# Storing three by three maxima instead of row maxima of five, and pooling every class of planes from them

## The chip, the cores and the metric

The kernel runs on one core of a Trainium2 chip. The metric is the device time of one execution in microseconds (us); runs are compared by their medians. The engines are named as in the profile: PE (matrix), DVE (vector), ACT (scalar), POOL (the fourth compute engine, which also issues the indirect DMAs) and SP (which issues the other DMAs).

## The reference

The input x has 16 images of 512 channels of 64 by 64 pixels, in float32. Layer 0 normalises x in groups of 16 channels, computes at each pixel the correlation with its 25 neighbours, divides these by their norm, and sends 512 + 25 channels through a one by one convolution with ReLU; its result is added to x and gives y. Layer 1 normalises y in groups and scores each of the 8192 planes (image and channel); the score picks two neighbouring pool sizes, and the result is their weighted sum. Cut to what matters here:

```
KERNELS = (1, 3, 5, 7, 9, 11, 13)
s = relu(score(b, c));  q_s = clip(floor(s), 0, 5);  q_b = q_s + 1
pools = [maxpool_same(y, k) for k in KERNELS]
y = y + (s - q_s) * pools[q_b] + (q_b - s) * pools[q_s] + groupnorm(y)
```

(The pools are taken of the normalised y, which is y scaled and shifted per plane with a positive factor, so the kernel takes them of y.)

## The kernel before

The second stage groups the planes by class q_s (0 to 5) into 67 tiles of 128 planes, one plane in a partition, and 5 empty tiles fill up to 72. The first stage makes y, and prepares for the second.

**First stage.** A loop over 16 images, each with 8 chunks of 8 rows (512 pixels for each of the 4 channel tiles of 128). Images 0, 14 and 15 are written out; the 13 between them are one turn of a DVE loop each, and PE's loop has a turn for seven. PE does for each chunk, in this order: `picks` (L1241), the products `gram` 0 and 1 of the next chunk (L1196), `tail` of the chunk before (L1274), `norm` (L1263), `gram` 2 and 3, one part of the convolution (L1219 to L1221), `turn_blocks` (L1254), and the other three parts. `gram` t waits until the mask of t - 2 is done, since two PSUM banks alternate: so `gram` 2 of a chunk waits for the first mask of that chunk.

DVE does for each chunk, in this order: `x_stats` (four BATCH_NORM_STATS2, L739; in all chunks but chunk 5), masks 0 and 1 (L789), `descriptor` (L831, L835, which wait for ACT's square root L617, which waits for `norm`), mask 2, the four `y_stats` (L801) with mask 3 between them, in chunk 0 `keep_stats`, in chunk 3 a second `x_stats`, then `wide_rows` for the chunk before, and in chunk 4 `group_spreads` and `group_values`, of which PE's `group_spread` (L1286) waits for L762. The y statistics wait for POOL's `residual` (L448), whose third and fourth part come after POOL's `halves`, which waits for `descriptor`. After `residual`, POOL does the subtraction L439 for the fourth channel tile of the chunk three ahead; those of the first three tiles come in the next chunk, as soon as ACT has made their inputs (L580, L582). In chunk 5 all four come behind `residual`.

`wide_rows` (L803) takes the maximum of five neighbours in a row, clamped at the ends, in six maxima over the 4 channel tiles at once (L810, L812, L817, L820, L822, L825). It puts pair maxima into `pairs_m`, whose space is shared with ACT's `relu`, and the result into the one buffer `wide`, which SP stores to `wide_planes` (L377, 1 MB). `s_middle` is raised after the third, `s_wide` after the last. The third waits for the store of the chunk before.

**Second stage.** For tile t, POOL gathers 128 planes of y (L507) and their records (L504) into one of four `bufs`, and the row maxima into one of two `source` buffers (L523), two tiles ahead; tiles of class 0 and 1 pool from y itself, and their `source` gather has out-of-range indices in all partitions but one, which fetch nothing. DVE's `pools` (all at L1039) makes the smaller pool in `small` and the larger in `big`, two buffers of each. ACT puts the scaled plane into the 8 PSUM banks (L665), PE adds diag times `small` (L1390; not in class 0) and diag times `big` (L1392) bank by bank, ACT copies the banks out (L679), and POOL scatters the result to `out` (L530). ACT takes tile t + 1 in only when all banks of tile t are out.

In class 0 `pools` takes seven maxima of half a plane and makes `big` (3 by 3). In class 1 two whole-plane maxima follow. In class 2 it makes five by five from the row maxima in four half-plane maxima, and then two whole-plane maxima for seven by seven. In classes 3 to 5 it widens the row maxima (three to six maxima), takes column maxima in `window`, and grows that by one. Outer rows and columns of `hbuf`, `small` and `source` are padded with the lowest float.

## Time and profile before

| | |
|---|---|
| median of 3 runs | 4183.77 us (4174.26 to 4189.22) |
| profiled execution: its time, its span | 4180.08 us, 4177.9 us |
| PE busy | 3474.2 us, 83% of the span |
| DVE busy | 3378.0 us, 81% |
| ACT, POOL busy | 1981.8 us, 2087.4 us |
| mean granted clock of PE | 0.919 of full |
| DMA moved | 782.10 MB, mean 187 GB/s |

The span runs from the first to the last instruction. The first stage ends at about 2550 us, the sorting of the planes at 2608 us, and the first maximum of the second stage starts at 2618.01 us. Busy times are shares of the whole span and mix the two stages; which engine is waited for has to be read in each stage by itself.

### The profile page before, as it was taken

The page shows a single profiled execution, that of the slowest core. Times are in us where ns is not written, and L with a number is a line of the kernel's source. Part 1 is how long each engine was busy: PE and PEld are TensorE (multiplying, and loading weights), DVE is VectorE, ACT ScalarE, POOL GpSimd, SP SyncE. Part 2 cuts the span into 40 slices and gives each one's busy share as a digit, 9 for nine tenths or more (in the row PEclk, how much of TensorE's full clock was granted, in tenths as well). Part 3 has the DMA queues.
Part 4 walks back from the last instruction along what each step waited for, and adds up shares of the span by engine and source line. Part 5 has one row for each costly group of instructions (what it writes and reads, how often), then busy time and mean ns, then how long its engine had stood idle before and what let it go on. Part 6 is the DMA issues. An engine that isn't in the chain of part 4 may idle for free. (4 is left out here: it accounts for less than half of the span.)

```text
span 4177.9 us, 72982 instructions
## 1 busy us (share of the span) xinstructions
PE 3474.2 (83%) x22600; PEld 1981.8 (47%) x22601; DVE 3378.0 (81%) x3619; ACT 1981.8 (47%) x3227; POOL 2087.4 (50%) x1576
## 2 busy tenths in 40 slices
PE   4999999999999999999999996567678666666554
PEld 3666666666665666666666664223233222222221
DVE  5777777777777777777777766899989999999995
ACT  3545445445445545545445440664556544444342
POOL 3555555556555555555555541554444444454343
PEclk9999999999999999999999996878889888877777
DMA  5445445445454454455455233664478666565552
GB/s 195 154 156 185 164 157 187 158 164 181 161 175 168 165 176 166 162 177 178 147 177 187 98 128 74 258 244 186 184 293 339 269 254 244 232 247 197 222 199 81
DMA packets 252355, 782.10 MB, mean 187 GB/s; under 512 B 98150, under 2 KB 98150, under 8 KB 229990
## 3 DMA queue, kind: packets, MB, share of 16 engines
q1 hardware_dynamic: 219600, 417.85, 29.0%
q0 software_dynamic: 32288, 358.95, 21.9%
q8 instruction: 181, 2.97, 0.3%
q14 instruction: 286, 2.34, 0.2%
HBM read 428.22 MB, written 409.08 MB: 200 GB/s over the span
## 5 line engine op out<-in xcount | busy, mean ns | idle before, releaser
L1039 DVE TENSOR_TENSOR arena<-arena 128x2048 f32<-128x2048 f32 (+9 forms) x635 | 1454.8, 2319 | 66.4 <-issue 23.1
L439 POOL TENSOR_TENSOR arena<-arena 128x512 f16<-128x512 f32 x512 | 651.2, 1277 | 861.5 <-ACT arena L582 860.3
L1390 PE MATMUL psum<-arena 128*128 128x512 f32 x896 | 534.9, 682 | 461.5 <-issue 336.6
L448 POOL TENSOR_TENSOR arena<-arena 128x512 f32 (+1 forms) x512 | 639.7, 1271 | 293.6 <-ACT arena L594 288.2
L1219 PE MATMUL psum<-arena 128*128 128x512 f16 x2048 | 776.3, 379 | 1.0 <-ACT arena L594 1.0
L1221 PE MATMUL psum<-arena 128*128 128x512 f16 x2048 | 776.2, 379 | 0.0
L1220 PE MATMUL psum<-arena 128*128 128x512 f16 x2048 | 776.2, 379 | 0.0
L1196 PE MATMUL psum<-arena 128*128 128x256 f16 (+1 forms) x6344 | 712.7, 270 | 34.5 <-DVE arena L789 21.2
L580 ACT ACTIVATE arena<-arena,gbias,grstd 128x512 f32 (+1 forms) x512 | 413.7, 808 | 632.0 <-PE psum L1221 515.6
L1392 PE MATMUL psum<-arena 128*128 128x512 f32 x1072 | 604.5, 661 | 71.1 <-ACT psum L665 54.4
L679 ACT ACTIVATE arena<-psum 128x512 f32<-128x512 f32 x536 | 315.9, 598 | 716.4 <-PE psum L1392 704.4
L1196 PEld LDWEIGHTS psum<-arena 128*128 128x128 f16 x6344 | 589.2, 99 | 118.9 <-DVE arena L789 29.4
L801 DVE BATCH_NORM_STATS2 bny<-arena 128x6 f32 (+1 forms) x512 | 354.3, 693 | 286.8 <-POOL arena L448 282.0
L530 POOL DMA_INDIRECT out<-arena x67 | 179.1, 2674 | 763.3 <-issue 763.3
L1390 PEld LDWEIGHTS psum<-arena 128*128 128x128 f32 x896 | 188.5, 218 | 724.3 <-issue 574.5
L594 ACT ACTIVATE arena<-psum,bias_sb 128x512 f32<-128x512 f32 x512 | 338.0, 686 | 217.7 <-POOL arena L448 205.8
L1392 PEld LDWEIGHTS psum<-arena 128*128 128x128 f32 x1072 | 230.3, 216 | 387.3 <-issue 320.9
L582 ACT ACTIVATE arena<-arena,gbias,grstd 128x512 f16 (+1 forms) x512 | 409.4, 800 | 0.0
L665 ACT ACTIVATE psum<-arena 128x512 f32<-128x512 f32 x536 | 383.3, 767 | 47.8 <-ACT arena L679 47.6
L739 DVE BATCH_NORM_STATS2 bnx<-arena 128x6 f32 (+1 forms) x512 | 314.8, 679 | 36.2 <-issue 25.2
L789 DVE TENSOR_TENSOR arena<-psum,cst 128x256 f32<-128x256 f32 x496 | 276.5, 587 | 79.3 <-PE psum L1196 78.9
L1221 PEld LDWEIGHTS psum<-arena 128*128 128x128 f16 x2048 | 200.4, 98 | 241.7 <-issue 0.2
(150 smaller groups left out, 3246.6 us busy)
## 6 DMA issues: line engine op xcount, KB each, us to landing
arena<-in_x SPq DMA_DIRECT2D x64, 2048.0 KB, 13.0
wide_planes<-arena SPq DMA_DIRECT2D x128, 1024.0 KB, 8.9
y_planes<-arena SPq DMA_DIRECT2D x64, 2048.0 KB, 7.7
arena<-arena SPq DMA_DIRECT2D x1536, 8.0 KB, 1.8
arena<-wide_planes,arena POOLq DMA_INDIRECT x72, 11.7
arena<-plane_records,arena POOLq DMA_INDIRECT x67, 7.8
arena<-y_planes,arena POOLq DMA_INDIRECT x67, 9.7
out<-arena POOLq DMA_INDIRECT x67, 9.2
```

The source lines that it names most:

```text
L439: pool.tensor_tensor(gl[:, ct, slot], g32[:, ct % 2, :], gh[:, ct, slot], ALU.subtract).then_inc(s_gl, 1)
L448: pool.tensor_tensor(y, y, relu[:, o % 2, :], ALU.add).then_inc(s_added, 1)
L580: act.activation(g32[:, ct % 2, :], piece, ACT.Identity, bias=gbias[:, ct:ct + 1], scale=grstd[:, ct:ct + 1])
L582: act.activation(gh[:, ct, (c % RING) * CW:(c % RING + 1) * CW], piece, ACT.Identity, bias=gbias[:, ct:ct + 1], scale=grstd[:, ct:ct + 1]) ...
L665: act.activation(psum[:, b, :], bufs[:, u, b * CW:(b + 1) * CW], ACT.Identity, bias=recs_in[:, u, 3:4], scale=recs_in[:, u, 0:1]).then_inc ...
L1039: ins = dve.tensor_tensor(dst, a, b, ALU.max)
L1196: return pe.matmul(dst, w, m, start=(k == 0), stop=(k == nk - 1))
L1219: pe.matmul(dst, h, gh[:, ct, slot], start=(ct == 0), stop=False)
L1220: pe.matmul(dst, h, gl[:, ct, slot], start=False, stop=False)
L1221: last = pe.matmul(dst, l, gh[:, ct, slot], start=False, stop=(ct == CT - 1))
L1390: pe.matmul(dst, diag[:, s, 0, :], small[:, s, b * ROWS:(b + 1) * ROWS, 1:W + 1], start=False, stop=False, skip_group_check=True)
L1392: pe.matmul(dst, diag[:, s, 1, :], big[:, s, b * CW:(b + 1) * CW], start=False, stop=True, skip_group_check=True).then_inc(s_mix, 1)
```

## The change

The first stage no longer stores row maxima of five, but three by three maxima, with the even columns of a row first and then the odd ones. Since the last row of a chunk needs the first of the next, chunk 0 stores 7 rows, chunk 7 stores 9, and the others 8 that start one row higher (`wide_span`). The work goes over two channel tiles at a time, and in chunk 7 over one, with seven maxima for each turn (eight in chunks 0 and 7): 14 maxima in chunks 1 to 6, 16 in chunk 0 and 32 in chunk 7. `column` takes the place of `pairs_m` in the space of `relu`. Every maximum of `wide_rows` now comes behind the wait for the store, and ACT waits for `s_wide` where it waited for `s_middle`.

In the second stage all classes gather these maxima, into three `source` buffers. Class 0 gives them to PE as they are, so that `pools` has nothing to do. Class 1 gives them to PE as the smaller pool and makes five by five with `grown` (one pixel wider on each side). Class 2 grows twice; classes 3 to 5 make seven, nine and eleven directly and grow that. PE reads planes in the split column order and writes each column to its place in PSUM, with a step of two elements. The diff, cut to its core:

```diff
-source = v(2 * (H + 2 * PADY) * W).rearrange("p (s h w) -> p s h w", s=2, w=W)
-hbuf_f = v((H + 2 * PADR) * W)
-hbuf = hbuf_f.rearrange("p (h w) -> p h w", w=W)
-small_f = v(2 * H * (W + 2))
-small = small_f.rearrange("p (s h w) -> p s h w", s=2, h=H)
-big = v(2 * PIX).rearrange("p (s n) -> p s n", s=2)
-half_m = v(36 * W)
+source = v(SRC * PIX).rearrange("p (s h w) -> p s h w", s=SRC, w=W)
+hbuf = v((H + 2) * W).rearrange("p (h w) -> p h w", w=W)
+small = v(2 * PIX).rearrange("p (s h w) -> p s h w", s=2, w=W)
+big = v(2 * PIX).rearrange("p (s h w) -> p s h w", s=2, w=W)
...
+def wide_span(c):
+    return max(c * ROWS - 1, 0), H if c == CH - 1 else (c + 1) * ROWS - 1
...
-        sp.dma_start(wide_v[bass.ds(i, 1), :, :, c * CW:(c + 1) * CW].rearrange("b p t n -> p (b t) n"),
-                     wide_f.rearrange("p (t n) -> p t n", t=CT)).then_inc(wide_stored, 16)
+        first, top = wide_span(c)
+        sp.dma_start(wide_v[bass.ds(i, 1), :, :, first * W:top * W].rearrange("b p t n -> p (b t) n"),
+                     wide_f.rearrange("p (t n) -> p t n", t=CT)[:, :, 0:(top - first) * W])\
+          .then_inc(wide_stored, 16)
...
-        sp.wait_ge(s_wide, i * CH + 2 * q + 2)
+        sp.wait_ge(s_wide, i * CH + min(2 * q + 3, CH))
...
-        if t >= 2:
-            pool.wait_ge(s_rows, t - 1)
-            pool.wait_ge(sourced[b % 2], t // 2 * 16)
-        pool.indirect_dma_start(out=source_flat(b % 2), out_offset=None, in_=wide_dram[:, :],
+    def gather_source(t):
+        if t >= SRC:
+            pool.wait_ge(sourced[t % SRC], t // SRC * 16)
...
-            act.wait_ge(s_middle, chunk)
+            act.wait_ge(s_wide, chunk)
...
+        def op(dst, a, b, wait=True, signal=s_pairs):
+            if wait and used[0]:
+                dve.wait_ge(s_pairs, n * PAIR_OPS + used[0])
+            dve.tensor_tensor(dst, a, b, ALU.max).then_inc(signal, 1)
+            if signal is s_pairs:
+                used[0] += 1
+        first, top = wide_span(c)
+        total = top - first
+        r = max(first, 1)
+        np_ = (min(top, H - 1) - r) // 2
         dve.wait_ge(s_added, (n + 1) * CT)
-        dve.tensor_tensor(pairs_m[:, :, :, 1:half], y[:, :, :, 1:W - 2:2], y[:, :, :, 2:W - 1:2], ALU.max)\
-            .then_inc(s_pairs, 1)
-        dve.tensor_tensor(pairs_m[:, :, :, 0:half + 1:half], y[:, :, :, 0:W:W - 1], y[:, :, :, 0:W:W - 1],
-                          ALU.max).then_inc(s_pairs, 1)
-        dve.wait_ge(s_pairs, n * 4 + 2)
         if not (isinstance(n, int) and n == 0):
             dve.wait_ge(wide_stored, n * 16)
-        dve.tensor_tensor(wide[:, :, :, 0:W:2], pairs_m[:, :, :, 0:half], pairs_m[:, :, :, 1:half + 1],
-                          ALU.max).then_inc(s_middle, 1)
-        dve.wait_ge(s_middle, n + 1)
-        dve.tensor_tensor(wide[:, :, :, 1:W - 2:2], wide[:, :, :, 0:W - 3:2], y[:, :, :, 3:W:2], ALU.max)\
-            .then_inc(s_pairs, 1)
-        dve.tensor_tensor(wide[:, :, :, W - 1:W], wide[:, :, :, W - 2:W - 1], wide[:, :, :, W - 2:W - 1],
-                          ALU.max).then_inc(s_pairs, 1)
-        dve.wait_ge(s_pairs, n * 4 + 4)
-        dve.tensor_tensor(wide[:, :, :, 2:W:2], wide[:, :, :, 2:W:2], y[:, :, :, 0:W - 3:2], ALU.max)\
-            .then_inc(s_wide, 1)
+        step = 1 if total > ROWS else 2
+        for t in range(0, CT, step):
+            ts = slice(t, t + step)
+            pairs = wide[:, ts, 0:np_, :]
+            column = relu_f[:, 0:step * total * W].rearrange("p (t h w) -> p t h w", t=step, w=W)
+            inner = column[:, :, r - first:r - first + 2 * np_, :]
+            op(pairs, y[:, ts, r:r + 2 * np_:2, :], y[:, ts, r + 1:r + 1 + 2 * np_:2, :])
+            op(inner[:, :, 0::2, :], pairs, y[:, ts, r - 1:r - 1 + 2 * np_:2, :])
+            op(inner[:, :, 1::2, :], pairs, y[:, ts, r + 2:r + 1 + 2 * np_:2, :], wait=False)
+            if c == 0:
+                op(column[:, :, 0:1, :], y[:, ts, 0:1, :], y[:, ts, 1:2, :], wait=False)
+            if c == CH - 1:
+                op(column[:, :, total - 1:total, :], y[:, ts, H - 2:H - 1, :], y[:, ts, H - 1:H, :], wait=False)
+            even, odd = wide[:, ts, 0:total, 0:W // 2], wide[:, ts, 0:total, W // 2:W]
+            op(odd, column[:, :, :, 0::2], column[:, :, :, 1::2])
+            op(even[:, :, :, 0:1], odd[:, :, :, 0:1], odd[:, :, :, 0:1])
+            op(even[:, :, :, 1:], odd[:, :, :, 1:], column[:, :, :, 1:W - 2:2], wait=False)
+            done = t + step == CT
+            op(odd[:, :, :, 0:W // 2 - 1], odd[:, :, :, 0:W // 2 - 1], column[:, :, :, 2::2],
+               signal=s_wide if done else s_pairs)
+        assert used[0] <= PAIR_OPS
+        dve.sem_inc(s_pairs, PAIR_OPS - used[0])
...
-        link(dve.tensor_scalar(sel, tcls, 2.0, None, ALU.is_ge))
-        link(dve.scalar_tensor_tensor(sel, tcls, float(NCLS), sel, ALU.is_lt, ALU.mult))
+        link(dve.tensor_scalar(sel, tcls, float(NCLS), None, ALU.is_lt))
...
+        def split(a):
+            return a.rearrange("p h (e j) -> p h e j", e=2)
+        def grown(src, dst, signal=s_own):
+            even, odd = split(src)[:, :, 0, :], split(src)[:, :, 1, :]
+            h_even, h_odd = split(inner)[:, :, 0, :], split(inner)[:, :, 1, :]
+            op(h_even[:, :, 1:], odd[:, :, 0:31], odd[:, :, 1:])
+            op(h_odd[:, :, 0:31], even[:, :, 0:31], even[:, :, 1:], wait=False)
+            op(h_even[:, :, 0:1], odd[:, :, 0:1], odd[:, :, 0:1], wait=False)
+            op(h_odd[:, :, 31:], even[:, :, 31:], even[:, :, 31:], wait=False)
+            op(dst, hbuf[:, 0:H, :], hbuf[:, 2:H + 2, :], signal=signal)
+        threes = source[:, u % SRC, :, :]
+        sm_, bg = small[:, s, :, :], big[:, s, :, :]
+        inner = hbuf[:, 1:H + 1, :]
+        even, odd = split(threes)[:, :, 0, :], split(threes)[:, :, 1, :]
+        h_even, h_odd = split(inner)[:, :, 0, :], split(inner)[:, :, 1, :]
+        def edge(a, n):
+            return a.to_broadcast([P, H, n])
+        def edge_row(r, n):
+            return inner[:, r:r + 1, :].to_broadcast([P, n, W])
+        if k == 2:
+            grown(threes, sm_)
+        elif k == 3:
+            m = split(bg)[:, :, 0, :]
+            tw = lambda a: a.rearrange("p h (e j) -> p (h e) j", e=2)
+            op(m[:, :, 1:31], odd[:, :, 0:30], even[:, :, 2:])
+            op(tw(inner)[:, :, 0:32:31], tw(threes)[:, :, 0:31:30], tw(threes)[:, :, 1:32:30], wait=False)
+            op(h_even[:, :, 1:31], m[:, :, 1:31], even[:, :, 0:30])
+            op(h_odd[:, :, 1:31], m[:, :, 1:31], odd[:, :, 2:], wait=False)
+            m = bg[:, 1:31, :]
+            two = lambda a: a.rearrange("p (a b) w -> p a b w", b=2)
+            op(m, inner[:, 1:60:2, :], inner[:, 4:63:2, :])
+            op(two(sm_)[:, 0:32:31, :, :], two(inner)[:, 0:32:31, :, :], two(inner)[:, 1:31:29, :, :], wait=False)
+            op(sm_[:, 2:61:2, :], m, inner[:, 0:59:2, :])
+            op(sm_[:, 3:62:2, :], m, inner[:, 5:64:2, :], wait=False)
+        elif k == 4:
+            m = split(bg)[:, :, 0, :]
+            op(m[:, :, 0:31], even[:, :, 0:31], odd[:, :, 1:])
+            op(h_odd[:, :, 0:1], odd[:, :, 0:1], even[:, :, 2:3], wait=False)
+            op(h_even[:, :, 31:], even[:, :, 31:], odd[:, :, 29:30], wait=False)
+            op(h_even[:, :, 2:31], m[:, :, 2:31], odd[:, :, 0:29])
+            op(h_odd[:, :, 1:30], m[:, :, 0:29], even[:, :, 3:], wait=False)
+            op(h_even[:, :, 0:2], m[:, :, 0:2], edge(odd[:, :, 0:1], 2), wait=False)
+            op(h_odd[:, :, 30:], m[:, :, 29:31], edge(odd[:, :, 31:], 2), wait=False)
+            m = bg[:, 0:31, :]
+            op(m, inner[:, 0:61:2, :], inner[:, 3:64:2, :])
+            op(sm_[:, 1:2, :], inner[:, 1:2, :], inner[:, 4:5, :], wait=False)
+            op(sm_[:, 62:63, :], inner[:, 62:63, :], inner[:, 59:60, :], wait=False)
+            op(sm_[:, 4:61:2, :], m[:, 2:31, :], inner[:, 1:58:2, :])
+            op(sm_[:, 3:60:2, :], m[:, 0:29, :], inner[:, 6:63:2, :], wait=False)
+            op(sm_[:, 0:3:2, :], m[:, 0:2, :], edge_row(1, 2), wait=False)
+            op(sm_[:, 61:64:2, :], m[:, 29:31, :], edge_row(63, 2), wait=False)
+        elif k == 5:
+            q_even, q_odd = split(bg)[:, :, 0, :], split(bg)[:, :, 1, :]
+            op(q_even[:, :, 0:31], even[:, :, 0:31], odd[:, :, 1:])
+            op(q_odd[:, :, 0:30], odd[:, :, 0:30], even[:, :, 2:], wait=False)
+            op(h_even[:, :, 2:30], q_even[:, :, 0:28], q_odd[:, :, 2:30])
+            op(h_odd[:, :, 2:30], q_odd[:, :, 0:28], q_even[:, :, 3:31], wait=False)
+            op(h_even[:, :, 0:2], q_odd[:, :, 0:2], edge(odd[:, :, 0:1], 2), wait=False)
+            op(h_odd[:, :, 0:2], q_even[:, :, 1:3], edge(odd[:, :, 0:1], 2), wait=False)
+            op(h_even[:, :, 30:], q_even[:, :, 28:30], edge(even[:, :, 31:], 2), wait=False)
+            op(h_odd[:, :, 30:], q_odd[:, :, 28:30], edge(even[:, :, 31:], 2), wait=False)
+            q = bg[:, 0:61, :]
+            op(q, inner[:, 0:61, :], inner[:, 3:64, :])
+            op(sm_[:, 4:60, :], q[:, 0:56, :], q[:, 5:61, :])
+            op(sm_[:, 0:4, :], q[:, 1:5, :], edge_row(1, 4), wait=False)
+            op(sm_[:, 60:64, :], q[:, 56:60, :], edge_row(62, 4), wait=False)
+        grown(threes if k == 1 else sm_, bg, signal=s_pool)
...
+                    if not (isinstance(t, int) and t < 2):
+                        dve.wait_ge(s_mix, (t - 1) * 8)
+                    dve.wait_ge(sourced[u % SRC], wide_loaded)
...
+                pe.wait_ge(sourced[u % SRC], wide_loaded)
+                mix_banks(t, s, [(1, threes)])
             with pe.Else():
-                mix_banks(t, u, s, True)
+                with pe.If(cls_t < 2):
+                    mix_banks(t, s, [(0, threes), (1, big[:, s, :, :])])
+                with pe.Else():
+                    mix_banks(t, s, [(0, small[:, s, :, :]), (1, big[:, s, :, :])])
...
-    def mix_banks(t, u, s, with_small):
+    def mix_banks(t, s, terms):
         for b in range(8):
             pe.wait_ge(s_first, t * 8 + b + 1)
-            dst = psum[:, b, :]
-            if with_small:
-                pe.matmul(dst, diag[:, s, 0, :], small[:, s, b * ROWS:(b + 1) * ROWS, 1:W + 1],
-                          start=False, stop=False, skip_group_check=True)
-            pe.matmul(dst, diag[:, s, 1, :], big[:, s, b * CW:(b + 1) * CW], start=False, stop=True,
-                      skip_group_check=True).then_inc(s_mix, 1)
+            dst = psum[:, b, :].rearrange("p (h j e) -> p h e j", h=ROWS, e=2)
+            for k, plane in terms:
+                rows = plane[:, b * ROWS:(b + 1) * ROWS, :].rearrange("p h (e j) -> p h e j", e=2)
+                last = pe.matmul(dst, diag[:, s, k, :], rows, start=False, stop=k == 1, skip_group_check=True)
+            last.then_inc(s_mix, 1)
```

## Rows read from the trace of the kernel before

**Rows 1.** Windows of the four stretches (columns as in the first row), core 0.
```profile
core 0: us, PE busy (x) PEld busy (x) DVE busy (x) ACT busy (x) POOL busy (x), PEclk, DMA share, GB/s
95.00:2540.00 2445.00, 2389.98 (x20125) 1498.31 (x20123) 1826.14 (x2772) 1184.62 (x1884) 1342.26 (x1256) 1.00 0.47 163
2618.00:2775.00 157.00, 89.73 (x160) 36.61 (x160) 150.16 (x77) 112.42 (x193) 82.31 (x39) 0.80 0.68 265
3278.00:4120.00 842.00, 517.70 (x1024) 217.93 (x1024) 811.97 (x379) 363.61 (x608) 387.31 (x128) 0.80 0.57 223
```

**Rows 2.** Timeline of DVE, a plain chunk: start, us, engine line, [idle before <-releaser].
```profile
1490.83 2.07 DVE L810 TENSOR_TENSOR arena<-arena 128x992 f32 x1
...
1493.23 1.23 DVE L817 TENSOR_TENSOR arena<-arena 128x1024 f32<-128x1024 f32 x1
1494.68 1.20 DVE L820 TENSOR_TENSOR arena<-arena 128x992 f32<-128x992 f32 x1 [0.22 <-DVE arena L817]
1495.79 0.22 DVE L822 TENSOR_TENSOR arena<-arena 128x32 f32<-128x32 f32 x1
1496.22 1.19 DVE L825 TENSOR_TENSOR arena<-arena 128x992 f32<-128x992 f32 x1 [0.20 <-DVE arena L822]
1497.33 2.46 DVE L739 BATCH_NORM_STATS2 bnx<-arena 128x6 f32 x4
1499.71 1.02 DVE L789 TENSOR_TENSOR arena<-psum,cst 128x256 f32<-128x256 f32 x2
```

**Rows 3.** Timeline of ACT: the square roots that follow norm, in four chunks.
```profile
1461.94 0.37 ACT L617 ACTIVATE arena<-psum,epsd 128x128 f32<-128x128 f32 x1 [0.30 <-PE psum L1263]
...
1482.98 0.37 ACT L617 ACTIVATE arena<-psum,epsd 128x128 f32<-128x128 f32 x1 [0.64 <-PE psum L1263]
...
1539.71 0.37 ACT L617 ACTIVATE arena<-psum,epsd 128x128 f32<-128x128 f32 x1 [0.17 <-PE psum L1263]
...
1560.86 0.37 ACT L617 ACTIVATE arena<-psum,epsd 128x128 f32<-128x128 f32 x1 [4.37 <-PE psum L1263]
```

**Rows 4.** Timelines of DVE and PE behind a turn of DVE's loop.
```profile
1457.66 1.19 DVE L825 TENSOR_TENSOR arena<-arena 128x992 f32<-128x992 f32 x1 [0.22 <-DVE arena L822]
1460.85 2.47 DVE L739 BATCH_NORM_STATS2 bnx<-arena 128x6 f32 x4 [2.00 <-issue]
1463.24 1.02 DVE L789 TENSOR_TENSOR arena<-psum,cst 128x256 f32<-128x256 f32 x2
...
1463.87 2.79 PE L1196 MATMUL psum<-arena 128*128 128x256 f16 x24 [1.97 <-DVE arena L789]
```

**Rows 5.** Timeline of DVE in chunk 4: the last row maximum and what PE waits for.
```profile
1553.04 1.19 DVE L825 TENSOR_TENSOR arena<-arena 128x992 f32<-128x992 f32 x1 [0.22 <-DVE arena L822]
...
1554.73 0.16 DVE L762 TENSOR_TENSOR gd<-gd,aggx 128x4 f32<-128x4 f32 x1
```

**Rows 6.** Timeline of POOL in the plain chunk of rows 2.
```profile
1490.70 1.16 POOL L439 TENSOR_TENSOR arena<-arena 128x512 f16<-128x512 f32 x1 [0.68 <-ACT arena L582]
1498.32 1.16 POOL L439 TENSOR_TENSOR arena<-arena 128x512 f16<-128x512 f32 x1 [6.46 <-ACT arena L582]
```

**Rows 7.** Timeline of DVE in the second stage: a tile of class 1, of class 2 in two parts.
```profile
2799.14 22.89 DVE L1039 TENSOR_TENSOR arena<-arena 128x2048 f32<-128x2048 f32 x9 [0.16 <-DVE arena L1039]
...
3149.24 9.21 DVE L1039 TENSOR_TENSOR arena<-arena 128x2112 f32<-128x2112 f32 x4
3158.60 8.88 DVE L1039 TENSOR_TENSOR arena<-arena 128x4096 f32<-128x4096 f32 x2 [0.15 <-DVE arena L1039]
```

**Rows 8.** Timeline of PE, two tiles of class 2.
```profile
3151.17 1.63 PE L1390 MATMUL psum<-arena 128*128 128x512 f32 x2 [2.21 <-ACT psum L665]
...
3165.84 1.02 PE L1392 MATMUL psum<-arena 128*128 128x512 f32 x2
3169.08 1.13 PE L1390 MATMUL psum<-arena 128*128 128x512 f32 x2 [2.22 <-ACT psum L665]
```

**Rows 9.** Windows: five microseconds in which DMA is full, columns as in rows 1.
```profile
3155.00:3160.00 5.00, 5.00 (x13) 2.25 (x12) 4.85 (x3) 3.52 (x8) 4.27 (x3) 0.99 1.02 387
```

**Rows 10.** Timeline of PE: products that write PSUM with a step.
```profile
1291.22 0.60 PE L1254 MATMUL psum<-cst,arena 128*128 128x128 f32 x4
...
1459.79 1.89 PE L1274 MATMUL psum<-arena 96*128 96x256 f16 x8
```

**Rows 11.** Store of the row maxima: all 128 of them, time from issue to landing.
```profile
DMA to landing us min/median/max: 4.2/8.9/16.2
```

136 lines of the change are left out of this document (28 added, 108 removed).

## The prediction

> **What bounds the kernel now.** I read the windows first, since the shares of the whole span mix two stages. In the first stage PE is busy 2390 of 2445 us at the full clock, DVE 1826 [rows 1]: PE is the bound, and the 619 us in which DVE idles look like room. In the second stage DVE is busy 812 of 842 us in classes 3 to 5 [rows 1], and its timeline has 0.15 us between tiles in classes 1 and 2 [rows 7]: there DVE is the bound. In class 2 PE follows closely, at one tile in 17.9 us (3151.17 to 3169.08) [rows 8] against DVE's 9.21 + 8.88 us and gaps, 18.4 [rows 7]. In class 0 DVE has 150 of 157 us and DMA a share of 0.68 [rows 1].
>
> Idle time is not room if it stands between two waits, so I read the timeline of one chunk for what comes after what. I name R the end of the square root L617. Five intervals carry the first stage:
> - R to the first row maximum: 7.5 us (1483.35 to 1490.83) [rows 2, 3]. It is a chain over ACT, POOL and DVE (ReLU, residual, halves, residual, statistics), which a faster or slower `wide_rows` doesn't touch. In chunk 0 `keep_stats` makes it 9.6, in chunk 3 the second `x_stats` 9.9.
> - `wide_rows` itself, W: 1490.83 to 1497.41, 6.6 us [rows 2].
> - its end to the end of mask 0: `x_stats` and one mask of 0.59, 1497.41 to 1500.3, 2.9 us [rows 2]; 5.0 behind the turn of DVE's loop (1458.85 to 1463.83) [rows 4].
> - mask 0 late: `gram` 2 starts as soon as it is done (1463.87, after 1.97 us idle), and the next R comes at 1483.35, 19.5 us behind the mask [rows 3, 4]. R itself is not late, since `norm` stands ahead of `gram` 2.
> - chunk 4: 7.0 us from the end of `wide_rows` (1554.23) to the next R (1561.23), since `group_spread` waits for L762, four small instructions behind it [rows 3, 5].
>
> When nothing is late, R comes every 18.9 us. So for two plain chunks in a row: 2 x 18.9 = 37.8 is the least, and 7.5 + W + 2.9 + 19.5 = 29.9 + W is what DVE allows. W may be 7.9 at most; now it is 6.6. That is all the room that the 619 us hold in a plain chunk. In chunk 4 there is none now.
>
> **First part: `wide_rows` is longer.** Before, 4096 elements in a partition in 6 maxima. After, chunks 1 to 6: per turn 512 x 4 + 16 + 496 x 2 = 3056, times 2 = 6112, in 14. One element takes 1/0.96 ns: 992 take 1.11 us when the next maximum doesn't wait (0.08 on top) and 1024 take 1.45 when it waits and forms an address in the loop (0.38 on top); a small one takes 0.43 [rows 2]. A wait without an address costs 0.19 on top, by the whole-plane maxima of the second stage (8.88 for two) [rows 7]. So 6.37 + 3 x 0.38 + 6 x 0.2 + 4 x 0.1 + 0.3 = 9.4 us without interference, where the old ones make 5.7. Chunk 0: 5212 elements, 8.7. Chunk 7 in four turns: 6748 elements and 32 maxima, 13.8.
>
> Interference is on top. L810 took 2.07 us here against 1.19 for L825 of as many elements, while L439 of POOL, begun at 1490.70, ran until 1491.86 [rows 2, 6]: 0.9 us. The next L439 begins at 1498.32, 0.9 us after the old `wide_rows` has ended, and well inside the new one. I take one further collision of 0.9 in each chunk that has subtractions there; the bounds are none and three. The Trainium skill (SBUF — State Buffer, Who interferes with whom) states that a DVE instruction with two SBUF inputs and a POOL instruction that reads SBUF exclude each other for a whole instruction. The 0.9 us agree. By that rule each of the three L439 (the third is due some 19 us after R) that meets the chain would cost a whole one, which is the upper bound here.
>
> In a plain chunk W is then 9.4 + 0.9 + 0.9 = 11.2, and 29.9 + 11.2 = 41.1 for two chunks instead of 37.8. With a late mask the 7.5 us are no longer exact: the chain through `descriptor` and `halves` gives 5.8 us from mask 0 to the first maximum, if that is later. Followed through one image (W; late mask after R; period): chunk 0: 14.7; 4.4; 23.9. Chunk 1: 9.6; 5.9; 25.4. Chunk 2: 11.2; none; 18.9. Chunk 3: 10.3; 2.7; 22.2. Chunk 4: 10.3; 1.8; 7.6 + 10.3 + 7.0 = 24.9. Chunk 5 (no `x_stats`, four subtractions): 12.8; none; 18.9. Chunk 6: 9.8; 4.3; 23.0. Chunk 7: 10.8; none; 19.1. Sum 176.3. The same rules give 153.6 for the old lengths. So +22.7 us for an image in the loop, +19.0 without a further collision (172.6), +30.8 with all three (184.4). For 13 images 295. In the three written out no addresses are formed (9.4 becomes about 8.8) and no loop turns: I estimate 14 each, 42, with the end, where the last `wide_rows` also waits for a store first. First stage: +337, bounds +280 and +450.
>
> The store moves in front of all maxima. It lands 4.2 to 16.2 us after issue, 8.9 in the median [rows 11]; with W at 11 it has 12 us or so until the next begins. The slow ones queue behind a load and a store issued earlier, so their landing stays where it is in time, and I cost it at nothing beside a late start; if they took their 15 us from the later issue, some 9 us an image, 120 in all. ACT's wait for `s_wide` costs nothing where mask 0 is late anyhow, since both wait for the same end. SP's loads wait for a chunk that the store issued before them has already waited for. Behind SP's wait for the store stand the regroup DMAs, which wait for `halves` some 3.5 us after R; even in chunk 1 the maxima end before that (26.9 - 23.9 = 3.0). The bytes stored stay the same.
>
> **Second part: `pools`.** `grown` is 2 x 1984, 2 x 64 and 4096 elements: 2.14 x 2 + 0.5 + 4.44 = 9.2 us [rows 2, 7].
> - Class 0: DVE does nothing. But a tile now moves three times 2.10 MB, 6.29 MB, where it moved two. DMA gives 387 GB/s when full [rows 9]: 16.3 us a tile; PE and ACT need about 10 (half of 15.7, and 2.2) [rows 8]. Before 14.4 (2618.0 to 2776.1, the latter from the first row of rows 7 less two tiles of class 1, for 11 tiles). The loss of 1.9 x 11 = 21 is given back by the start, where 14 us of maxima no longer stand before PE's first product, and by 8 products at the end: together -2. The Trainium skill (SBUF — State Buffer, A bandwidth-pool intuition that's wrong) gives 358 GB/s for HBM to a core; that would be 17.6 us a tile and 14 us more in all. The 387 of the trace stands against it.
> - Class 1: DVE 9.4, DMA 16.3, PE and ACT 17.6 (17.9, and half a microsecond less in a tile that starts at the full clock, as 1.13 stands to 1.63 in rows 8). Against 22.89 + 0.16 [rows 7]: 11 x 5.5 = -61.
> - Class 2: 18.5 against 18.4: +1.
> - Classes 3, 4, 5: with elements/0.96 and 0.15 for each maximum, 20224, 20352 and 24192 elements in 13, 19 and 17 maxima make 23.0, 24.15 and 27.9 us. The old sizes by the same rule make 24.6, 25.65 and 28.4, which gives 837 of the 842 us window [rows 1]. So 11 x -1.6, 11 x -1.5, 10 x -0.5: -39.
> PE's longer way through the branches and the fewer paddings are under 2 us and cancel. Second stage: -2 - 61 + 1 - 39 = -101, bounds -80 and -130 (class 1 at the 16.3 of DMA).
>
> **PE writes PSUM with a step of two.** L1274, in f16, writes with a step: 8 products of 256 columns take 1.89 us, where 24 of L1196 without one take 2.79 [rows 4, 10], so 0.22 against 0.11 each. L1254, in f32, has a step of 16 and takes 0.11 us for 128 columns (0.60 for 4, the last 0.27 long) [rows 10], 0.85 ns a column, as the f32 records of the mix do (15.7 us for 32 of 512 columns, 0.43 at the full clock) [rows 8]. The mix is f32, nearest to L1254: no cost. The other bound is a rival.
>
> **The sum.** 4180.1 + 337 - 101 = 4416. The profiled execution is 3.7 us (0.1%) below the median of the runs shown, so I keep 4415, +5.5%. 0.3% is about what a measurement of this kernel tells from no change.
>
> **The rivals.**
> - Faster: the longer `wide_rows` fits into DVE's 619 us, and PE keeps 18.9. For it: 128 x 3.7 = 474 us is less than 619. Against it: the place of the idle time, and `gram` 2 that already waited 1.97 us for a mask [rows 4]. It decides where W is under 7.9 in a plain chunk, and 6112 elements take 6.4 us without any overhead. Then 4183.8 - 101 = 4083. Chance 0.10.
> - Half the loss: part of the 7.5 us chain or of `x_stats` gives way. +15 an image and 25, 220 in all less 101: 4300. Chance 0.10.
> - All subtractions collide, or the stores land 15 us behind their later issue, or PE's longer idle time lowers its clock (it was 1.00 in the first stage and 0.80 in class 0, where PE idles 40% [rows 1]): 4183.8 + 450 - 101 = 4530. Chance 0.16.
> - The step costs PE double: 27.4 + 2.2 = 29.6 us for each tile of classes 1 to 5, so 12, 11, 6.6, 5.5 and 1.7 us more on 11, 13, 11, 11 and 10 tiles, 426 in all: 4840. Chance 0.10.
> - My forecast, 4415, by itself 4350 to 4480: 0.54.
>
> The range 4250 to 4540 leaves out the first and the fourth. Faster by over 0.3% 0.10, within 0.3% 0.02, slower 0.88.
>
> **What the changed profile would show.** The first stage is right if L739 starts directly behind the last maximum, PE idles ahead of `gram` 2 in chunks 0, 1, 3 and 6, L617 comes every 22 us in the mean, and PE waits 5 us or more for L762; wrong if PE is busy 98% there. W is right at 9.4 to 11.2. The second stage is right if the DMA share is near 1 in class 0, tiles of class 1 take 17.6 us with DVE half idle, and a pair of products stays at 1.02. What would make it wrong most easily is W, since each microsecond of it is worth half a microsecond in a plain chunk and a whole one in chunk 4.

## Result and the profile after

The changed kernel takes 4628.84 us (median of 4 runs, 4624.27 to 4631.09) against 4185.63 (median of 4, 4174.26 to 4189.22): a ratio of 1.106 (95% interval 1.104 to 1.109). The forecast was 4415, in a range of 4250 to 4540. The direction was right, the size was not. The profiled execution took 4631.09 us, with a span of 4629.3; before, 4180.08 and 4177.9.

Windows of the changed kernel: the first stage, class 0, classes 3 to 5, and below them a wait of PE, the four microseconds behind it, and five later ones of the same chunk. Columns as in [rows 1].

```profile
core 0: us, PE busy (x) PEld busy (x) DVE busy (x) ACT busy (x) POOL busy (x), PEclk, DMA share, GB/s
95.00:3060.00 2965.00, 2520.06 (x19833) 1565.18 (x19832) 2385.01 (x4028) 1180.49 (x1867) 1344.44 (x1237) 0.91 0.37 133
3196.00:3342.00 146.00, 92.69 (x155) 37.88 (x156) 0.00 (x0) 101.42 (x182) 37.30 (x37) 0.75 1.00 420
3760.00:4585.00 825.00, 536.21 (x1061) 226.44 (x1062) 797.88 (x533) 380.78 (x638) 348.21 (x136) 0.81 0.60 239
1818.00:1826.00 8.00, 0.00 (x0) 0.00 (x0) 6.93 (x16) 2.00 (x4) 2.47 (x3) 0.69 0.43 168
1826.00:1830.00 4.00, 3.62 (x18) 2.56 (x19) 2.66 (x6) 0.88 (x2) 2.41 (x4) 0.50 0.33 122
1838.00:1843.00 5.00, 5.00 (x68) 2.48 (x66) 4.30 (x10) 0.32 (x1) 0.15 (x1) 1.00 0.99 364
```

From the first R to the last, the first stage takes 3018.0 us instead of 2451.7, 566 more. (The windows can't be subtracted for this: this one ends 26 us before the last R, that of [rows 1] 20 us behind it.) In the windows PE is no longer busy 98% of the time but 85%. DVE is busy 2385 us and still idles 580: neither engine is full in the mean, as before. The waits say who stops whom. Waits of PE, 200 to 3000 us: line waited for, total, times, longest.

```profile
PE psum L1203 <- DVE arena L786: 397.5, 72, 8.6
PE psum L1293 <- DVE gd L759: 31.9, 14, 3.0
```

L1203 is `gram` (L1196 before), L786 the mask (L789), L1293 `group_spread`. In 72 chunks PE stands before `gram` 2 for the first mask, 5.5 us in the mean.

One plain chunk, timelines of DVE, POOL, PE and ACT. The maxima of `wide_rows` are now L812, the subtraction L440, the square root L614, `x_stats` L736.

```profile
1660.53 0.69 DVE L798 BATCH_NORM_STATS2 bny<-arena 128x6 f32 x1 [0.54 <-POOL arena L449]
1661.14 1.59 DVE L812 TENSOR_TENSOR arena<-arena 128x512 f32 x1
1662.94 3.54 DVE L812 TENSOR_TENSOR arena<-arena 128x512 f32<-128x512 f32 x6 [0.21 <-DVE arena L812]
1667.21 0.69 DVE L812 TENSOR_TENSOR arena<-arena 128x512 f32 x1 [0.73 <-DVE arena L812]
1668.11 6.17 DVE L812 TENSOR_TENSOR arena<-arena 128x512 f32<-128x512 f32 x6 [0.21 <-DVE arena L812]
1674.20 2.47 DVE L736 BATCH_NORM_STATS2 bnx<-arena 128x6 f32 x4
1676.58 1.02 DVE L786 TENSOR_TENSOR arena<-psum,cst 128x256 f32<-128x256 f32 x2
```
```profile
1661.02 1.16 POOL L440 TENSOR_TENSOR arena<-arena 128x512 f16<-128x512 f32 x1 [0.70 <-ACT arena L579]
1668.64 1.19 POOL L440 TENSOR_TENSOR arena<-arena 128x512 f16<-128x512 f32 x1 [6.46 <-ACT arena L579]
1670.05 1.34 POOL L440 TENSOR_TENSOR arena<-arena 128x512 f16<-128x512 f32 x1 [0.23 <-ACT arena L579]
1671.66 1.28 POOL L440 TENSOR_TENSOR arena<-arena 128x512 f16<-128x512 f32 x1 [0.28 <-ACT arena L579]
```
```profile
1677.21 3.17 PE L1203 MATMUL psum<-arena 128*128 128x256 f16 x14 [5.05 <-DVE arena L786]
```
```profile
1653.27 0.37 ACT L614 ACTIVATE arena<-psum,epsd 128x128 f32<-128x128 f32 x1 [0.63 <-PE psum L1270]
1672.20 0.37 ACT L614 ACTIVATE arena<-psum,epsd 128x128 f32<-128x128 f32 x1 [0.61 <-PE psum L1270]
1698.17 0.37 ACT L614 ACTIVATE arena<-psum,epsd 128x128 f32<-128x128 f32 x1 [0.54 <-PE psum L1270]
```

The five intervals of the prediction can be read off. R is 1653.64 (1653.27 + 0.37), the first maximum comes 7.5 us later, `wide_rows` lasts to 1674.28, so W = 13.1, the mask is done at 1677.2, 2.9 behind it and 4.6 behind the next R (1672.57); `gram` 2 waited 5.05 us. All four subtractions lie inside `wide_rows`. The R after that comes at 1698.54, 26.0 us after its predecessor, while the pair started with one of 18.9. The mean of the 13 images in the loop, from the first R of one to the first R of the next, is 194.3 us (before: 155.3; the prediction's rules gave 176.3 and 153.6).

The second stage, from the last R to the end of the span, takes 1542.9 us instead of 1657.8: 115 us less. Tiles of class 1, timeline of DVE (L1055 is every maximum of `pools`) and PE (L1402, both products):

```profile
3368.57 9.25 DVE L1055 TENSOR_TENSOR arena<-arena 128x1984 f32<-128x1984 f32 x5 [6.25 <-DMA arena<-wide_planes,arena]
3384.04 9.24 DVE L1055 TENSOR_TENSOR arena<-arena 128x1984 f32<-128x1984 f32 x5 [6.22 <-DMA arena<-wide_planes,arena]
```
```profile
3381.80 14.00 PE L1402 MATMUL psum<-arena 128*128 128x512 f32 x32 [2.22 <-ACT psum L662]
```

DVE is busy 9.25 us in a tile where it was 22.89 [rows 7]. PE's 32 products take 14.0 us with the step of two, at a granted clock of 1.00; in the kernel before the 32 of the tile of class 2 that starts at 3169.08 take 14.0 us without the step, at 1.00 as well.

### The profile page after: what moved, and what is told of

Read it like the earlier page. It is cut to its first block and busy times, and to the rows that moved or that the text cites. A ratio compares the mean times of both kernels' runs of the same rounds, so it can differ in the third digit from the quotient of the medians.

```text
span 4629.3 us, 75558 instructions
## 1 busy us (share of the span) xinstructions
PE 3626.9 (78%) x22600; PEld 2064.7 (45%) x22601; DVE 3642.6 (79%) x5029; ACT 1976.8 (43%) x3227; POOL 2003.2 (43%) x1576
## 5 line engine op out<-in xcount | busy, mean ns | idle before, releaser
L812 DVE TENSOR_TENSOR arena<-arena 128x512 f32<-128x512 f32 (+11 forms) x2112 | 1392.8, 686 | 150.8 <-DVE arena L812 102.7
L1055 DVE TENSOR_TENSOR arena<-arena 128x64 f32<-128x64 f32 (+8 forms) x707 | 1119.5, 1636 | 275.5 <-DMA arena<-wide_planes,arena 210.8
L1402 PE MATMUL psum<-arena 128*128 128x512 f32 x1968 | 983.5, 663 | 421.8 <-ACT psum L662 266.8
L1203 PE MATMUL psum<-arena 128*128 128x256 f16 (+1 forms) x6344 | 855.6, 302 | 421.8 <-DVE arena L786 409.0
L440 POOL TENSOR_TENSOR arena<-arena 128x512 f16<-128x512 f32 x512 | 666.1, 1304 | 1095.7 <-ACT arena L579 1093.9
L1203 PEld LDWEIGHTS psum<-arena 128*128 128x128 f16 x6344 | 660.7, 110 | 579.3 <-DVE arena L786 423.7
L1402 PEld LDWEIGHTS psum<-arena 128*128 128x128 f32 x1968 | 414.5, 214 | 990.7 <-issue 706.4
L676 ACT ACTIVATE arena<-psum 128x512 f32<-128x512 f32 x536 | 305.0, 603 | 547.9 <-PE psum L1402 535.3
L591 ACT ACTIVATE arena<-psum,bias_sb 128x512 f32<-128x512 f32 x512 | 337.9, 686 | 379.0 <-POOL arena L449 205.6
L527 POOL DMA_INDIRECT out<-arena x67 | 167.2, 2495 | 749.2 <-issue 749.2
L798 DVE BATCH_NORM_STATS2 bny<-arena 128x6 f32 (+1 forms) x512 | 338.6, 682 | 134.5 <-POOL arena L449 131.5
L786 DVE TENSOR_TENSOR arena<-psum,cst 128x256 f32<-128x256 f32 x496 | 276.4, 587 | 196.6 <-PE psum L1203 196.5
L736 DVE BATCH_NORM_STATS2 bnx<-arena 128x6 f32 (+1 forms) x512 | 314.9, 678 | 38.2 <-issue 27.2
L1228 PEld LDWEIGHTS psum<-arena 128*128 128x128 f16 x2048 | 201.3, 98 | 244.7 <-issue 5.4
L1226 PEld LDWEIGHTS psum<-arena 128*128 128x128 f16 x2048 | 203.5, 99 | 215.3 <-issue 4.7
```

Of the source, the lines that this page charges most:

```text
L440: pool.tensor_tensor(gl[:, ct, slot], g32[:, ct % 2, :], gh[:, ct, slot], ALU.subtract).then_inc(s_gl, 1)
L812: dve.tensor_tensor(dst, a, b, ALU.max).then_inc(signal, 1)
L1055: ins = dve.tensor_tensor(dst, a, b, ALU.max)
L1203: return pe.matmul(dst, w, m, start=(k == 0), stop=(k == nk - 1))
L1226: pe.matmul(dst, h, gh[:, ct, slot], start=(ct == 0), stop=False)
L1228: last = pe.matmul(dst, l, gh[:, ct, slot], start=False, stop=(ct == CT - 1))
```

## The experiments

In the table "pace" is the mean time of an image over the 13 in the loop, read from the square roots of each trace, and "W, sum" the lengths of the eight `wide_rows` of an image added up, in the same 13 (in e6 those of its halves). e1, e2 and e4 are one execution each; repeated runs of one kernel here stay within 0.5% of each other.

| run | us | pace | W, sum | from last R to the end |
|---|---|---|---|---|
| before | 4181 to 4186 | 155.3 | 53.7 | 1657.8 |
| changed | 4628.8 | 194.3 | 97.9 | 1542.9 |
| e1, before, one maximum twice | 4259.6 | 161.9 | 65.8 | 1646.4 |
| e2, before, one maximum four times | 4648.3 | 187.0 | 93.5 | 1662.3 |
| e3, changed, half the maxima | 4069.6 | 155.4 | 42.5 | 1539.6 |
| e4, changed, no subtraction | 4345.3 | 175.1 | 77.8 | 1546.5 |
| e5, changed, later `x_stats` | 4525.6 | 187.2 | 98.1 | 1546.7 |
| e6, e5 and half of `wide_rows` later | 4522.9 | 185.3 | 91.1 | 1545.2 |
| e7, e5 without subtraction | 4279.6 | 170.8 | 77.8 | 1544.6 |
| e8, changed, filler on PE | 4603.6 | 192.4 | 99.3 | 1542.5 |
| e9, changed, long filler | 4614.0 | 191.4 | 99.3 | 1544.1 |
| e10, before, no subtraction | 4169.8 | 154.7 | 48.2 | 1658.1 |

**Is it the length of `wide_rows`?** Two doses on the kernel before. One of its maxima is repeated, with the same operands and result:

```diff
+for j in range(1):          # e2: 3
+    dve.wait_ge(s_pairs, n * 5 + 4 + j)
+    dve.tensor_tensor(wide[:, :, :, 1:W - 2:2], wide[:, :, :, 0:W - 3:2], y[:, :, :, 3:W:2], ALU.max)\
+        .then_inc(s_pairs, 1)
```

> The kernel before, with one of the six maxima of wide_rows (L820, 992 elements in a partition) made a second time with the same values, so W grows by about 1.5 us, to 8.1. The store, its wait and ACT's wait for s_middle stay as they are. Theory (DVE works in order, so a longer wide_rows makes mask 0 late once W is over 7.9 in a plain chunk, and at once in chunk 4): 5 to 9 us more for an image, 4260 to 4340 in all, and PE waiting for masks by several times the 1.97 us of a chunk that it waited before. Rival (DVE has 619 us of room in the first stage): 4184. Rival (what cost time in the changed kernel is the wait for the store or ACT's wait for s_wide, not the length): 4184.

> The kernel before, with the maximum L820 made four times in place of once, W about 11.1 us, as long as in the changed kernel. Theory: about 19 us more for an image without collisions with POOL and 30 with them, so 4490 to 4700, and in a plain chunk with a late mask the square root comes 19.5 us or more behind mask 0. If the drop of PE's granted clock belongs to the idle time, it shows here too (below 0.95 in the first stage). Rivals as in the run with one repetition: 4184 both.

Measured: 4259.6 and 4648.3 us, one execution each, beside 4181.8 for the kernel before (median of 7). What PE waits for, from 200 to 2400 us, first with one repetition, then with three:

```profile
PE psum L1200 <- DVE arena L789: 82.3, 39, 2.3
PE psum L1290 <- DVE gd L762: 10.0, 6, 1.7
```
```profile
PE psum L1200 <- DVE arena L789: 247.1, 62, 6.4
PE psum L1290 <- DVE gd L762: 43.1, 11, 4.5
```

Unchanged, the kernel before has 21.2 us of the first wait in the same window, 24 times. With nothing but a longer `wide_rows` it loses 78 and 466 us, the first 0.4 us below the range expected, the second inside it. Both rivals gave 4184 and fall. With three repetitions the granted clock of PE is 0.93 in the first stage, below 0.95 as expected. The slope is instructive. The first repetition makes `wide_rows` 12.0 us longer in an image and costs 6.7; the next two make it 27.8 us longer (two maxima in each of eight chunks are some 24, the rest is waits and subtractions that now lie beside it) and cost 25.0. Below the room of 7.9 us a part is free; over it a microsecond of W costs 0.9, not the half that the prediction put on a plain chunk. At 93.5 us of W this kernel has a pace of 187.0, and the changed one with 97.9 has 194.3: length explains most of the loss.

**Do the waits cost, or the maxima?** The changed kernel with the maxima of channel tiles 2 and 3 alone, all waits and stores kept:

```diff
-for t in range(0, CT, step):
+for t in range(CT // 2, CT, step):
```

> The changed kernel, with the maxima of the first stage made for channel tiles 2 and 3 alone (in chunk 7 the same), so that W is about 5 us; the other half of wide_planes holds zeros, and the output is not the reference's. Every wait and every store stays. Theory (the loss is the length of wide_rows): the first stage takes as long as before, and the second keeps its gain of about 125 us: 4040 to 4080. Rival (the wait for the store in front of all maxima, or ACT's wait for s_wide, cost time by themselves): over 4150. The second stage by itself: 120 to 130 us less than before.

Measured: 4069.6 us, ratio 0.974 (0.972 to 0.975), within what was expected. The pace is that of before. So the wait for the store in front of all maxima, the loads that wait longer, and ACT's wait for `s_wide` cost nothing where W is short (42.5 us an image). The run doesn't show what they cost at the full W, since a short W also gives the store more time to land and ends ACT's wait early. The second stage, from the last R, is 118 us shorter by itself; 120 to 130 were expected.

**The subtractions.** The changed kernel with L440 made for 8 of 512 columns:

```diff
-pool.tensor_tensor(gl[:, ct, slot], g32[:, ct % 2, :], gh[:, ct, slot], ALU.subtract).then_inc(s_gl, 1)
+few = slice((c % RING) * CW, (c % RING) * CW + 8)
+pool.tensor_tensor(gl[:, ct, few], g32[:, ct % 2, 0:8], gh[:, ct, few], ALU.subtract).then_inc(s_gl, 1)
```

> The changed kernel, with the subtraction of POOL (L440) made for 8 of 512 columns; the rest of the low parts is zero, so the convolution is less precise and the output is not the reference's. It takes away the work of POOL that runs beside the maxima of DVE and nothing else. Theory (each of the subtractions that meets wide_rows costs DVE 0.9 us, three or more in a plain chunk): W falls from about 11.2 to 9.4 us, an image gets 12 us shorter or more, 4380 to 4450 in all. Rival (waits and addresses make W long, POOL does not matter): W stays over 10.5 and the time over 4580.

Measured: 4345.3 us (one execution), 283 less than the changed kernel and below the range expected. The same chunk of the same image as above, timeline of DVE (L817 are the maxima, L741 `x_stats`):

```profile
1510.93 0.68 DVE L817 TENSOR_TENSOR arena<-arena 128x512 f32 x1
1511.82 3.55 DVE L817 TENSOR_TENSOR arena<-arena 128x512 f32<-128x512 f32 x6 [0.21 <-DVE arena L817]
1516.09 0.69 DVE L817 TENSOR_TENSOR arena<-arena 128x512 f32 x1 [0.73 <-DVE arena L817]
1517.00 3.57 DVE L817 TENSOR_TENSOR arena<-arena 128x512 f32<-128x512 f32 x6 [0.21 <-DVE arena L817]
1520.49 2.46 DVE L741 BATCH_NORM_STATS2 bnx<-arena 128x6 f32 x4
```

W is 9.6 instead of 13.1. The lines that differ are those over which a subtraction lay: 0.68 against 1.59, one subtraction; 3.57 against 6.17, three. Each adds 0.87 to 0.91 us. Over all 2112 maxima, first the changed kernel, then this one:

```profile
L812 DVE TENSOR_TENSOR arena<-arena 128x512 f32<-128x512 f32 (+11 forms) x2112 | 1392.8, 686 | 150.8 <-DVE arena L812 102.7 <-DMA wide_planes<-arena 9.5 <-issue 6.0
```
```profile
L817 DVE TENSOR_TENSOR arena<-arena 128x512 f32<-128x512 f32 (+11 forms) x2112 | 1089.3, 542 | 177.7 <-DVE arena L817 102.6 <-DMA wide_planes<-arena 36.6 <-issue 5.8
```

303.5 us less, 19.0 for each of the 16 images (W in the loop falls by 20.0), and the pace falls by 19.2. The two lines also show DVE's wait for the store: 9.5 us in all in the changed kernel, and 36.6 in this one, where DVE is ready for it earlier. So the collisions hid a part of that wait, and it is small in both.

**The control on the kernel before.** The same edit there.

> The kernel before, with POOL's subtraction (L439) made for 8 of 512 columns; the rest of the low parts is zero, and the output is not the reference's. In the changed kernel that took 19.2 us off an image. Theory (a subtraction costs only through wide_rows, and only where W is over the room): here W falls from 6.6 to about 5.7 in a room of 7.9, so plain chunks gain nothing, and chunk 4 and the turn of the loop gain 1 us each or less: 153 to 155 us an image against 155.3, 4145 to 4185 in all. Rival (the subtractions cost time of their own, on ACT or PE, whatever wide_rows is): over 10 us an image, under 4030.

Measured: 4169.8 us, ratio 0.997 (0.996 to 0.998), a pace of 154.7 against 155.3. POOL's subtraction is the same work in both kernels; it is worth 0.6 us an image where `wide_rows` fits its room (W falls by 5.5 in sum, and nearly all of that is free) and 19.2 where it doesn't. The time and the pace lie within what was expected.

**The order on DVE.** `x_stats` goes from the front of mask 0 to between the masks and statistics behind `descriptor`:

```diff
-if c < 5 and left >= 1:
-    x_stats(i + 1, c + 2 if c < 4 else CH - 1)
...
+if c < 4 and left >= 1:
+    xs_ = [lambda ct=ct: x_stats(i + 1, c + 2, (ct,)) for ct in range(CT)]
...
+between = [between[0], between[1] + xs_[0:1], between[2] + xs_[1:2],
+           between[3][0:1] + xs_[2:4] + between[3][1:]]
```

> The changed kernel, with the four x_stats of a chunk moved from the front of masks 0 and 1 to places behind descriptor, between mask 2, mask 3 and the first y_stats, where DVE waits for POOL; the x_stats of chunk 4 and the second ones of chunk 3 stay. From the end of wide_rows to mask 0 there is then one mask, 0.6 us, instead of 2.9. Theory (what counts is how late mask 0 is, and it is late by the length of what DVE does behind y_stats): the room for W in a plain chunk grows from 7.9 to 10.2 us, an image gets 9 to 19 us shorter, and the time is 4330 to 4480. Rival (DVE is simply full, since its work for a chunk fills the period, and its order does not matter): over 4580.

> The kernel with the later x_stats, and with POOL's subtraction made for 8 of 512 columns (the rest of the low parts is zero, the output is not the reference's). W is then 9.3 us and the room 10.2, so by the theory plain chunks keep PE's 18.9 us, and only chunks 0, 3, 4 and 7 lose: 163 to 168 us for an image and 4180 to 4270 in all. If the two causes (length of the work ahead of mask 0, collisions) were not what matters, it would stay near the 4345 us of the run without the subtraction alone.

Measured: 4525.6 us, ratio 1.083 (1.079 to 1.087), and without subtractions 4279.6, ratio 1.024 (1.020 to 1.027). The first lies between the ranges of the two theories, 103 us better than the changed kernel; the second is 10 us over its range. The order matters, by 7.1 us an image of the 9 to 19 expected. Two things take the rest back. Where the mask is late, DVE has few waits behind it for `x_stats` to fill: in one chunk 3 the first maximum of e5 comes 10.2 us after mask 0 (9.6 to 11.2 in the 13 of the loop), and in the changed kernel 9.3. And what one chunk gains the next returns, because R comes earlier and DVE does not: without subtractions chunk 3 goes from 20.6 to 18.9 us by the move (e4 and e7, from its R to the next, means of 12 images), and chunk 4 from 24.9 to 26.4. DVE being full is a part of the truth, and the rival named it.

**Half of `wide_rows` behind the masks.** On top of e5:

```diff
-wide_rows(i, c - 1)
+wide_rows(i, c - 1, 0)                            # tiles 0 and 1, at the old place
...
+sums = [lambda: wide_rows(i, c - 2, 1)] + sums    # tiles 2 and 3, between mask 1 and descriptor
```

> The kernel of the run before, and wide_rows cut in two: channel tiles 0 and 1 at the old place, tiles 2 and 3 behind masks 0 and 1 of the next chunk, ahead of descriptor. Masks 0 and 1 then never wait for more than half of wide_rows. The work is the same. Theory: no mask is late, but DVE has about 20.5 us of work for a chunk with collisions, and descriptor is late instead; the period goes to that, some 164 to 172 us an image, PE idles in pieces short enough to keep its clock, and the time is 4200 to 4350. Rival (the order does not matter): over 4580. Rival (the second half delays descriptor, and with it the store, ReLU and residual, by more than it spares): 4450 to 4600.

Measured: 4522.9 us, ratio 1.082 (1.079 to 1.085), the same as e5. What PE waits for, 200 to 2400 us (L1244 is the first product of a part of the convolution, L1279 `turn_blocks`, L591 the ReLU):

```profile
PE psum L1244 <- ACT arena L591: 254.8, 95, 5.5
PE psum L1279 <- DVE arena L787: 31.4, 44, 1.0
```

`gram` no longer waits for masks, as planned (in the changed kernel it does so for 321.7 us in this window), and another wait stands in the place of that one, nearly as large: `column` lies in the space of `relu`, so ReLU waits for `s_wide`, and the next convolution, which writes the PSUM that ReLU reads, waits for ReLU. In the changed kernel the profile shows no such wait of PE; that the late mask 0 covered it there is the reading that fits, and no run tests it alone. The third expectation (the second half delays what follows `descriptor`) is the one that came. A buffer of its own for `column` was not tried.

**The clock of PE.** The windows above show 0.69 while PE idles for 8 us, then 0.50, that is 1.2 GHz, and 1.00 again later. The first `gram` behind that wait, in the changed kernel:

```profile
1826.38 5.13 PE L1203 MATMUL psum<-arena 128*128 128x256 f16 x24 [8.55 <-DVE arena L786]
```

24 products in 5.13 us, not 2.79 [rows 4]. Behind late masks R comes 1.6 to 2.4 us later than the 19.5 of the prediction (than 18.7 in chunk 6, as in the kernel before); with 1.5 in chunk 4 that is about 10 us an image. Whether that is 10 us of the loss is another question. Products with a tile of zeros, which add nothing, fill the wait in chunks 0, 1, 3 and 6:

```diff
+if fill:
+    for k in range(40):      # e9: 64, 72, 40 and 48 in chunks 0, 1, 3 and 6
+        ins = pe.matmul(psum[:, CT - 1, 0:256], zw, wh[:, 0, 0:256], start=False, stop=True, skip_group_check=True)
+    ins.then_inc(s_conv, 1)  # in place of the one at the end of tail's fourth part
```

> The changed kernel, with 40 more products on PE, of 256 columns in f16, between norm and gram 2 in chunks 0, 1, 3 and 6, where PE waits 5 to 8.7 us for mask 0. They multiply by a tile of zeros and add into the PSUM of the fourth part of the convolution, so the result stays what it is; at the full clock they take about 4.3 us and lie in the wait. Theory (the 10 us an image that the loss exceeds the sum with all collisions come from PE's granted clock, which is 0.5 behind a long wait): behind the filler the clock stays up, the square root comes 19.5 us behind a late mask in place of 21.1 to 21.8, and the image gets 6 to 9 us shorter: 4490 to 4550 in all. Rival (the extra time behind a late mask is not the clock but DVE or ACT being late with something else): 4620 or more.

> As the run with the filler on PE, with 64, 72, 40 and 48 products in chunks 0, 1, 3 and 6, so that the wait for mask 0 is filled nearly whole in all four and the clock behind it should stay at the full one. Theory A (the lower clock is in series with the rest, and the first filler was too short in chunks 0 and 1): the square root comes 19.5 us behind the late mask there too, the image goes from 192.4 to 185 to 188 us, 4500 to 4550 in all. Theory B (DVE is the bound once its masks are late in most chunks, so what the clock gives back to PE makes the next mask later by nearly as much): 190 to 192.5 us an image, 4570 to 4610.

Measured: 4603.6 us, ratio 1.101 (1.099 to 1.102), between the two ranges given for it, and 4614.0, ratio 1.104 (1.102 to 1.106), 4 us over the range of theory B, whose pace it meets (191.4). It is slower in all than the first filler although its pace is 1.0 us better, since the three images written out take 13 us more. With the long filler, the same chunk 1 as above, timeline of PE (L1318 is the filler):

```profile
1802.38 8.02 PE L1318 MATMUL psum<-arena 128*128 128x256 f16 x72
1811.09 2.79 PE L1206 MATMUL psum<-arena 128*128 128x256 f16 x24 [0.69 <-DVE arena L789]
```

The clock is back: 24 products take 2.79 us again. Means over 12 images of the time from the R of a chunk to the next, changed kernel and long filler: chunk 1, 29.96 and 27.69; chunk 3, 25.97 and 24.14; chunk 6, 26.95 and 24.54. But chunk 4 goes from 27.85 to 30.17 and chunk 7 from 19.09 to 21.01. Of 7.2 us given back in chunks 0, 1, 3 and 6, some 4.2 are lost again one chunk later, since R comes earlier while DVE does not, so the next mask is late by so much more.

In chunk 0 the test isn't clean. There the long filler outlasts the wait: mask 0 is done 4.2 us after R, the filler ends 6.6 us after R, `gram` 2 starts without a wait, and DVE and ACT wait in turn. Timelines of ACT (L593 is the ReLU, which the filler's end releases) and DVE:

```profile
1783.78 0.69 ACT L593 ACTIVATE arena<-psum,bias_sb 128x512 f32<-128x512 f32 x1 [3.70 <-PE psum L1318]
```
```profile
1784.99 0.60 DVE L789 TENSOR_TENSOR arena<-psum,cst 128x256 f32<-128x256 f32 x1 [2.07 <-PE psum L1206]
```

In chunks 1, 3 and 6 R comes 19.5, 19.5 and 18.7 us behind mask 0, as at the full clock; in chunk 0 it comes 21.3 behind it. Even if those last 1.8 us were all given back, the image would take 189.6 us, and not the 185 to 188 of theory A. The half clock in chunk 4, which had no filler, wasn't tested. Theory A and its estimate for the first filler fall, theory B fits the pace: DVE is the bound through most of an image, and PE's lower clock is in the main a symptom.

None of these is faster than the kernel before and computes the reference: the best that do are e5 and e6, at 1.08. With the two largest causes reduced at once (e7) it is still 1.02.

## Why the prediction was wrong

- **What bounds the kernel.** Right: the length of `wide_rows`, the order in DVE and the late first mask, not DVE's share. e1, e2 and e3 show the length, e5 a part of the order.
- **W without interference.** 9.4 us for chunks 1 to 6 was forecast, 8.7 for chunk 0 and 13.8 for chunk 7; without subtractions it is 9.6 in the chunk shown and mostly 9.3, 8.5 and 13.5.
- **Collisions: the step that failed.** "I take one further collision of 0.9 in each chunk that has subtractions there; the bounds are none and three." Price right (0.87 to 0.91), number wrong. In the chunk shown the subtractions come 7.4, 15.0, 16.4 and 18.0 us after R. The old `wide_rows` ended at 14.1, ahead of the last three; the new one would end at 17.1 without collisions (e4) and reaches 20.6 with four. Two of the three further subtractions meet it whatever they cost; only the last needs the stretch that the others add. All this could be read before: the prediction had "the third is due some 19 us after R", but in the trace of the kernel before they start 15.0, 16.4 and 18.0 us after the R at 1483.35. Timeline of POOL, behind the two of [rows 6]:

```profile
1499.73 1.16 POOL L439 TENSOR_TENSOR arena<-arena 128x512 f16<-128x512 f32 x1 [0.25 <-ACT arena L582]
1501.32 1.15 POOL L439 TENSOR_TENSOR arena<-arena 128x512 f16<-128x512 f32 x1 [0.43 <-ACT arena L582]
```

  With the first collision alone the prediction's own chain ends 7.5 + 9.4 + 0.9 = 17.8 us after R, behind two of them; with those two added it ends at 19.6, behind the third. Not every chunk is at the upper bound: against e4, W is 3.5 us longer in chunk 2, 5.1 in chunk 5, 3.0 in chunk 7, 3.7 in chunk 0, 2.3 in chunk 3, and 0.8 in chunks 1, 4 and 6. In the prediction's own rules its collisions are worth about 8.3 us an image (176.3 less the 168.0 that the rules give with none, an estimate worked out as the prediction did), and all three further ones 16.4 (184.4); e4 measured 19.2. The rule of the Trainium skill (SBUF — State Buffer, Who interferes with whom) that was set beside it names the right pairs: all four that met the chain cost something. A whole exclusion is more than was seen, though: 0.87 to 0.91 us each, where the subtractions took 1.16 to 1.34.
- **What a microsecond of W costs.** "Half a microsecond in a plain chunk and a whole one in chunk 4" is right for a late mask followed by a chunk without one. Here late masks follow each other (chunks 3 and 4; 0 and 1 behind a 7 with little slack), and then it is nearly one for one: 25.0 for 27.8 us from e1 to e2, 19.2 for 20.0 in e4.
- **The clock: the second term that failed.** The sum has it at nothing, with R always 19.5 us behind a late mask; measured were 21.1 to 21.9 in chunks 0, 1, 3 and 6. e4 shows it too: without a collision an image takes 175.1 us, where the rules give 168.0 (1.7 of that gap they have for the kernel before too, 153.6 for 155.3). It was put into a rival, as an alternative to the collisions ("all subtractions collide, or the stores land 15 us behind, or PE's longer idle time lowers its clock"), at 4530 in sum. Both came together. The sum of 184.4 with all collisions and 10 for the clock hits the 194.3 measured, but that doesn't prove it: with the clock back the image takes 191.4 and not 184.4. Of the 10 us the long filler gave back 3.0 (the first 1.9); behind most of the rest stands DVE, whose masks are late by as much. How much a filler that is right in chunks 0 and 4 would give stays open.
- **The first stage in numbers.** Forecast +337. Measured from first to last R: +566, which is 13 x 39.05 = 508 for the images in the loop, where 295 was forecast, and 58 for the others with the start, where 42 was.
- **Chunk 4.** 27.85 us, forecast 24.9. The first maximum comes 9.3 us after R and not 7.6, since the mask is late by 2.4 and not 1.8 and the first maximum comes 6.9 us behind it and not 5.8. The 7.0 us from `wide_rows` to R became 8.5 with the idle time before `group_spread`, again the half clock (`picks`: 1.51 us in place of 0.88).
- **The store, ACT's wait, the loads.** Costed at nothing; the store's part is right by the 9.5 us in the line of L812, and e3 shows no cost at a short W. The cover was plausibly named (both wait for the same end): when e6 moves the masks ahead, ACT's wait holds PE for 255 us between 200 and 2400.
- **The second stage.** Forecast -101, bounds -80 and -130; -115 measured from the last R. Split at PE's first product of a class: up to class 0 +2, class 0 -5, class 1 -61, class 2 -2, classes 3 to 5 -49. Class 0: 14.65 us a tile, not 16.3, because DMA moves 420 GB/s in the window of class 0 and not the 387 taken from five microseconds of another class. But the 14 us at the start were not gained: the two errors cancel, and the -2 forecast for class 0 with its start came out at -3 by luck. Class 1: the -61 forecast, at 17.05 us a tile for 17.6. Class 2: -2, forecast +1. Classes 3 to 5: -49 instead of -39, with tiles of 23.3, 23.7 and 27.5 us (forecast 23.0, 24.15 and 27.9; by the prediction's own rule the last two are 24.05 and 27.75). Its 2776.1 is the first row of [rows 7] less one tile of class 1, not two; the 14.4 us a tile are right.
- **The step of two in PSUM.** No cost, as forecast: 32 products in 14.0 us with it and without it. The rival at 4840 is out.
- **The rivals.** "Faster, 4083" comes near what e3 shows (4070), for a first stage that this `wide_rows` doesn't allow. Of the signs named for the first stage, PE's idle time ahead of `gram` 2 came as said; R comes every 24.3 us in the mean and not every 22, W is 12.2 in the mean and not 9.4 to 11.2, and PE waits 2.3 us in the mean for the instruction before `group_spread` (31.9 us in 14 times), not 5 or more. The 216 us between the forecast and the profiled execution are the images in the loop (+213), the others (+17) and the second stage (-14).

## What to carry to other kernels

Where a cost depends on whether two things overlap, take the start of each from the trace and hold it against the end of the stretch, with the costs counted so far added; a middle value between the bounds throws away what the trace already says. Where the cost lengthens the stretch, go through once more, since it may reach the next one. An engine with 20% idle time can be the bound, and past its room a microsecond costs nearly a whole one; a dose of dummy work in the kernel at hand measures both the room and the slope before anything is rebuilt. Two effects that need the same condition are not alternatives to be given one chance.

## What the runs showed of the hardware

- DMA moved 420 GB/s over 146 us in class 0, with three streams of whole planes, reads and writes together; the 387 of [rows 9] was no ceiling. (In PE's first tile of class 1, 3363.99 to 3379.57, it was 423.) The 358 GB/s of the Trainium skill that the prediction set beside it (SBUF — State Buffer, A bandwidth-pool intuition that's wrong) are passed. The Trainium skill (HBM Reference, Specifications (TRN2)) has about 425 GB/s for a core that streams alone; this window agrees.
- The granted clock of PE in chunk 4 of the changed kernel was 1.00 from 1709.0 to 1716.4, 0.99 while PE waited until 1718.6, and 0.50 in the two microseconds behind. Timeline of PE:

```profile
1718.60 0.59 PE L1293 MATMUL psum<-gd,cst 128*128 128x4 f32 x2 [2.23 <-DVE gd L759]
1719.11 1.51 PE L1248 MATMUL psum<-arena,cst 128*32 128x64 f32 x48
```

  The 48 products of `picks` take 1.51 us; in the kernel before, in the same place behind a wait of 1.54 us, they took 0.88 at a granted clock of 1.00.
- In e4 the tiny subtractions cost DVE nothing that its lines show (3.57 us for six maxima, with two of them beside), though one took 0.65 us for 8 columns where others took 0.20. Timeline of POOL:

```profile
1518.43 0.65 POOL L445 TENSOR_TENSOR arena<-arena 128x8 f16<-128x8 f32 x1 [7.41 <-ACT arena L584]
1519.84 0.20 POOL L445 TENSOR_TENSOR arena<-arena 128x8 f16<-128x8 f32 x1 [0.76 <-ACT arena L584]
```

  So the subtractions of 512 columns cost DVE 0.87 to 0.91 us each and those of 8 columns nothing visible. That the 0.65 us is POOL waiting out a maximum of DVE is a reading of this one row; it is not shown by a run of its own.
